# A sorted mixture-of-experts layer: the slot table inverted by one-hot matmuls, token rows gathered straight into SBUF, token weights applied in the combine

## What is computed

```
logits = x @ gate_w.T
scores = jax.nn.softmax(logits, axis=-1)
topk_w, topk_idx = jax.lax.top_k(scores, K)
topk_w = topk_w / jnp.sum(topk_w, axis=-1, keepdims=True)
h = jnp.einsum('th,ehi->eti', x, w1)
g = jnp.einsum('th,ehi->eti', x, w3)
y_all = jnp.einsum('eti,eih->eth', jax.nn.silu(h) * g, w2)
y_sel = y_all[topk_idx, tok]
y = jnp.sum(y_sel * topk_w[..., None], axis=1)
shared = jax.nn.silu(x @ sw1) * (x @ sw3) @ sw2
return (y + shared).reshape(hidden_states.shape)
```

## Time and profile before

| | us |
|---|---|
| median of 3 executions | 1532.87 |
| lowest, highest | 1524.81, 1533.39 |
| the profiled execution, its own time | 1529.62 |
| its span in the trace | 1527.5 |
| PE, DVE, ACT, POOL busy in the span | 1244.4, 954.8, 718.1, 449.8 |

### The profile page before, as it was taken

How to read it: one execution, slowest core, us unless ns; L and a number is a source line. 1 busy time by engine, 2 the same in 40 slices (tenths; PEclk the granted TensorE clock), 3 DMA queues, 4 the chain that set the end, 5 groups by cost and what they waited for, 6 DMA issues and landing times.

```text
span 1527.5 us, 24987 instructions
## 1 busy us (share of the span) xinstructions
PE 1244.4 (81%) x7159; PEld 933.5 (61%) x7195; DVE 954.8 (63%) x2322; ACT 718.1 (47%) x1364; POOL 449.8 (29%) x479
## 2 busy tenths in 40 slices
PE   4579795699765888888869999999789999997466
PEld 3358794577543544545546666666578888885344
DVE  7765454444578999899952445453564555455986
ACT  3452463333336888888842444432423333323275
POOL 3278345200004656565632111210200011003400
PEclk9889897899978999999965999996899999998589
DMA  7645345201011111110100000000000000210001
GB/s 218 124 137 168 111 126 173 62 18 52 1 41 43 42 42 42 42 42 1 35 8 7 8 8 14 0 18 4 21 21 21 21 21 21 87 51 14 1 15 42
DMA packets 72500, 73.36 MB, mean 48 GB/s; under 512 B 10603, under 2 KB 67710, under 8 KB 72414
## 3 DMA queue, kind: packets, MB, share of 16 engines
q1 hardware_dynamic: 69006, 62.98, 14.2%
q0 software_dynamic: 3408, 9.34, 1.7%
HBM read 53.62 MB, written 18.68 MB: 47 GB/s over the span
## 4 chain that ended last, share of the span: by engine, by line
PE 42%; DVE 15%; issue 8%; ACT 6%; POOL 2%; DVEq 0%; ACTq 0%; POOLq 0%
PE bank L935 11%; PE bank L956 5%; PE bank L2505 4%; PE bank L2544 4%; PE bank L2534 3%; DVE work L2041 2%; PE bank L2068 2%; PE bank L2491 2%; DVE work L2031 2%; PE bank L2082 1%; PE bank L2560 1%; DVE resid L2058 1%; PE bank L2075 1%; PE bank L2484 1%; PE bank L2941 1%
## 5 line engine op out<-in xcount | busy, mean ns | idle before, releaser
L2037 POOL TENSOR_TENSOR work<-work 128x512 f32<-128x512 f32 x128 | 163.1, 1275 | 166.6 <-DVE work L2031 166.6
L2068 PE MATMUL bank<-work 128*128 128x512 bf16 x481 | 129.1, 389 | 7.2 <-DVE work L2031 3.8
L2082 PE MATMUL bank<-work 128*128 128x256 bf16 x512 | 78.2, 275 | 38.2 <-ACT work L2025 24.3
L935 PE MATMUL bank<-xhi,whi 128*128 128x512 f32 x256 | 102.2, 399 | 6.1 <-PE bank L956 3.4
L2082 PEld LDWEIGHTS bank<-work 128*128 128x128 bf16 x512 | 41.5, 97 | 100.4 <-issue 96.7
L935 PE MATMUL bank<-xlo,whi 128*128 128x512 f32 x256 | 101.2, 395 | 0.0
L935 PE MATMUL bank<-xhi,wlo 128*128 128x512 f32 x256 | 100.9, 394 | 0.0
L2031 DVE TENSOR_TENSOR work<-work,bank 128x512 f32<-128x512 f32 x128 | 86.4, 676 | 18.6 <-ACT work L2014 15.0
L2020 ACT ACTIVATE work<-work 128x512 f32<-128x512 f32 x128 | 91.7, 716 | 6.0 <-DVE work L2051 5.7
L822 POOL TENSOR_TENSOR wlo<-raw,whi 128x1536 fp32r<-128x1536 f32 x8 | 28.1, 3509 | 224.1 <-ACT whi L836 224.1
L876 DVE TENSOR_TENSOR work<-work,bank 128x512 f32<-128x512 f32 x64 | 44.0, 688 | 78.4 <-PE bank L935 77.6
(11 more groups left out here) (448 smaller groups left out, 3414.1 us busy)
## 6 DMA issues: line engine op xcount, KB each, us to landing
f_got<-f_sorted SPq DMA_DIRECT2D x39, 129.0 KB, 2.1
f_sorted<-clear_row SPq DMA_DIRECT2D x1, 4992.0 KB, 23.5
raw<-in_L_ffn_w SPq DMA_DIRECT2D x24, 176.0 KB
f_back<-f_outputs SPq DMA_DIRECT2D x16, 256.0 KB, 3.0
ctx_in<-in_ctx SPq DMA_DIRECT2D x32, 128.0 KB, 2.0
raw<-in_L_ffn_W SPq DMA_DIRECT2D x14, 256.0 KB, 3.2
f_lines<-f_tokens SPq DMA_DIRECT2D x12, 256.0 KB, 3.7
resid<-in_x SPq DMA_DIRECT2D x4, 512.0 KB, 8.2
```

The source lines that it names most:

```text
L935: mm = pe.matmul(bank[2 * mat + u % 2][0:m, :], up_w(w, slot, mat, c, q), x[:, c, cols], start=j == 0, stop=j == 3 * DC - 1)
L2037: pool.tensor_tensor(prod[:, t % RING, :], once[:, t % 2, :], relu[:, t % RELUS, :], ALU.mult).then_inc(s.prod, 1)
L2068: mm = pe.matmul(bank[2 * m + t % 2][:, :], xqT[:, c, t * P:(t + 1) * P], up_w[:, slot, m, c, :], start=c == 0, stop=c == DC - 1)
L2082: mm = pe.matmul(bank[6 + t % 2][:, 0:D], wholeT[:, t % 2, c * P:(c + 1) * P], down_w[:, slot, c, :], start=c == 0, stop=c == IC - 1)
```

## The change

- The DRAM tensor `f_sorted`, its clearing at the start of the program, the reload of the rows, the payload copies and the 32 scatters into it go.
- VectorE builds a one-hot row matrix [token, 128] and a one-hot column matrix [token, 2 x 39] per choice (`vector_hot`, twice four instructions) after units 2 and 3. TensorE multiplies them (`tensor_inverse`, 32 matmuls, after `tensor_up(5)`). That gives for each of the 39 x 128 slots the token that fills it. VectorE makes from it the source row and the destination row (`vector_slots`, seven small instructions, after unit 5).
- GpSimd gathers the rows of each sorted tile from `f_tokens` straight into a ring of 16 in SBUF (`gather`), 4 in flight: 16 gathers ahead of the tile loop, and one gather behind each of the first 23 scatters in it.
- ScalarE's copy of the output has no weight. The combine has no GpSimd in it: VectorE does two multiply-adds per tile, with the token's weight, in a staggered order.
- The small tables move: GpSimd makes some at the start of the program, VectorE makes others (`vector_tables`) before the first `vector_shift`; the route weights are made after the first `vector_shift` instead of after the fourth. `layer1_weights.load` is issued when the tile loop begins, no longer after its last load.

```
+        def tables_gpsimd(pool):
+            pool.memset(all_one[:, :], 1.0).then_inc(made, 1)
+            pool.iota(count_int[:, :], [[1, P]], base=0, channel_multiplier=0).then_inc(made, 1)
+            pool.iota(row_int[:, :], [[0, 1]], base=1, channel_multiplier=1).then_inc(made, 1)
...
+            def vector_tables(dve):
...
+                link(dve.memset(maskb[:, TILES, :], 0.0))
+                link(dve.tensor_scalar(by_rank, counting[:, 0:E], -1.0, float(E), ALU.mult, ALU.add))
+                link(dve.tensor_scalar(at_tile, counting[:, 0:NT], float(P), None, ALU.mult))
+                link(dve.tensor_scalar(pad_place, at_tile, row1[:, :], float(K * TOK), ALU.add, ALU.add))
...
+                link(dve.tensor_scalar(high, value, (1 - P) / 2.0, 1.0 / P, ALU.add, ALU.mult))
+                link(dve.tensor_scalar(high, high, MAGIC, None, ALU.add))
+                link(dve.tensor_scalar(high, high, MAGIC, None, ALU.subtract))
+                link(dve.scalar_tensor_tensor(low, high, -float(P), value, ALU.mult, ALU.add))
...
+            def vector_hot(dve, k):
+
+                dve.tensor_tensor(rows[k], counting[:, :].unsqueeze(1).to_broadcast([P, TILES, P]),
+                                  low[:, k, :].unsqueeze(2).to_broadcast([P, TILES, P]), ALU.is_equal).then_inc(p.hot, 1)
+                n = [P, TILES, NT]
+                dve.tensor_tensor(columns[k][:, :, 0, :], counting[:, 0:NT].unsqueeze(1).to_broadcast(n), high[:, k, :].unsqueeze(2).to_broadcast(n),
+                                  ALU.is_equal).then_inc(p.hot, 1)
+                dve.wait_ge(p.hot, 4 * k + 2)
+                dve.tensor_tensor(columns[k][:, :, 1, :], columns[k][:, :, 0, :],
+                                  counting[:, k * TILES:(k + 1) * TILES].unsqueeze(2).to_broadcast(n), ALU.mult).then_inc(p.hot, 1)
+                dve.wait_ge(p.hot, 4 * k + 3)
+                dve.tensor_scalar(columns[k][:, :, 0, :], columns[k][:, :, 0, :], row1[:, :], None, ALU.mult).then_inc(p.hot, 1)
...
+            def tensor_inverse(pe):
+                hold(pe, p.hot, 4 * K)
+                for k in range(K):
+                    for t in range(TILES):
+                        mm = pe.matmul(inverse, rows[k][:, t, :], columns[k][:, t, :, :], start=k + t == 0, stop=k == K - 1 and t == TILES - 1)
+                mm.then_inc(p.inverse, 1)
...
+                pool.wait_ge(p.slots, 2)
+                for i in range(2):
+                    pool.wait_ge(p.kept[i], 16 * 2)
+
+                def gather(j):
+                    if j >= FLIGHT:
+                        pool.wait_ge(sent[j % FLIGHT], moved_up_to(j - FLIGHT))
+                    if j >= IN_RING:
+                        pool.wait_ge(s.in_ps, j - IN_RING + 1)
+                    pool.indirect_dma_start(got[:, j % IN_RING, :], None, tokens,
+                                            bass.IndirectOffsetOnAxis(ap=sorter.token[:, j:j + 1], axis=0)).then_inc(sent[j % FLIGHT], 16)
+                for j in range(IN_RING):
+                    gather(j)
                 for j in range(NT):
-                    pool.wait_ge(s.lo, j + 1)
+                    pool.wait_ge(s.out, j + 1)
...
+                    if j + IN_RING < NT:
+                        gather(j + IN_RING)
...
-                        act.activation(y_out[:, i % OUT_RING, :], bank[6 + i % 2][:, 0:D], ACT.Copy,
-                                       scale=got[:, i % IN_RING, D + 1:D + 2]).then_inc(s.out, 1)
+                            act.wait_ge(gone[i % FLIGHT], moved_up_to(i - OUT_RING))
+                        act.activation(y_out[:, i % OUT_RING, :], bank[6 + i % 2][:, 0:D], ACT.Copy).then_inc(s.out, 1)
...
+                for x in range(TILES + K):
+                    for k in range(K):
+                        t = x - k
+                        if 0 <= t < TILES:
+                            if k:
+                                dve.wait_ge(s.acc[k - 1], t + 1)
+                            else:
+                                dve.wait_ge(s.back[t % OUT_RING], 16 * (t // OUT_RING + 1))
+                            dve.scalar_tensor_tensor(X[:, t, :], y_back[:, t % OUT_RING, k, :], sorter.share[:, k, t:t + 1], X[:, t, :],
+                                                     ALU.mult, ALU.add).then_inc(s.acc[k], 1)
+                    if x >= K:
+                        dve.wait_ge(s.acc[K - 1], x - K + 1)
+                        next_stat(dve, x - K)
...
-            steps_at = {1: ("pay", "places"), 3: ("which",), 5: ("powers",), 7: ("series",), 9: ("weights",)}
+            steps_at = {1: ("pay", "places"), 2: ("hot0",), 3: ("hot1",), 5: ("slots", "which"), 7: ("powers",), 8: ("series",), 9: ("weights",)}
```

More of the change, by code:

```diff
@@ L1043, in sorted_experts @@
                 p.up1, p.up2, p.silu, p.hid, p.ahi, p.alo, p.down, p.acc,
-                p.ones, p.mask, p.ranks, p.chain, p.paid, p.where, p.which, p.lined, p.rows0, p.rows1, p.rows2, p.rows3
+                p.mask, p.ranks, p.chain, p.which, p.hot, p.inverse, p.slots
             ) = late.of("kept0 kept1 raw hi0 lo0 stage0 stage1 stage2 hi hi_late lo shift up1 up2 silu hid ahi alo down acc "
-                        "ones mask ranks chain paid where which lined rows0 rows1 rows2 rows3")
-            p.kept, p.stage, p.rows = (p.kept0, p.kept1), (p.stage0, p.stage1, p.stage2), (p.rows0, p.rows1, p.rows2, p.rows3)
@@ L1048, in sorted_experts @@
-            STAGES = 3
+                        "mask ranks chain which hot inverse slots")
+            p.kept, p.stage = (p.kept0, p.kept1), (p.stage0, p.stage1, p.stage2)
             s = Names()
             (
-                s.here0, s.here1, s.here2, s.here3, s.in_ps, s.hi, s.lo, s.up, s.silu, s.act, s.turn_ps, s.ahi, s.alo, s.down, s.out,
-                s.back0, s.back1, s.back2, s.back3, s.pair, s.acc
-            ) = early.of("here0 here1 here2 here3 in_ps hi lo up silu act turn_ps ahi alo down out "
-                         "back0 back1 back2 back3 pair acc")
@@ L1107, in sorted_experts @@
+            columns = [over(f"{name}_columns{k}", work_at, at["columns"][k], [P, TILES, 2, NT], F16)[:, :, :, :] for k in range(K)]
             small, lay = taker(small_area, 512), taker(scratch, at["scratch_size"])
-            pay = small(TILES, K, 2)
-            value, index = small(K, TILES), small(K, TILES, dt=U32)
-            tiles_of, first, end = small(E), small(E), small(E)
-            weights_of, dest = small(NT, dt=I32), small(NT, dt=U32)
             router = make_router(name, split, lay, None, 0, E, K, gate, *router_args, lean=True)
-            logits = router.logits
```

423 lines of the change are left out of this document (204 added, 219 removed).

## The result

The changed kernel takes 1538.6 us (median of 20), the kernel before 1532.6 (median of 20): ratio 1.0039, 95% interval 1.0025 to 1.0054. That is no change by the bound of 1%, and a loss of some 6 us that twenty executions can tell. Forecast 1537.5. Medians are taken over all executions, while ratios and intervals leave out those that ran clearly longer at a lower clock (4 of the 20 after the change), so a ratio isn't always the quotient of the two medians.

What follows compares the result with a forecast made beforehand. TensorE was taken to bound the shared expert and tile loop, a DMA, GpSimd and VectorE chain the combine. Terms summed to +6.95 on the profiled 1529.6, giving 1536.6; forecast put at 1537.5 us, range 1524 to 1551.

Steps and rivals of the forecast that it cites:

- The one-hot matrices: Shared expert: VectorE's wide steps, 4.4 us per choice, make TensorE's `tensor_down(4)` late by +5.9 us.
- The clock in the shared expert: Shared expert: two new TensorE waits of about 2 us, one clock fall taken, +1.3 us, bounds 0 to +2.5.
- From the shared expert to the tile loop: Between shared expert and loop: last scatter and load go, gathers land in time, so the gap goes, -4.4 us.
- The warm clock at loop fill: Loop's start: TensorE idles 1.8 us instead of 6.2, so less low clock, -1.3 us, bounds -2.6 to 0.
- The tile loop: Loop: GpSimd falls behind 0.41 us per tile, 23 times; ring of 4 and TensorE's slack absorb part, +3.1 us.
- The combine: Combine: three-step chain through the ring, 1.39 us a tile against 1.05, +3.3 us, bounds +1 to +5.
- The small tables: Layer's start: GpSimd's low part comes earlier without its seven table operations, -0.95 us, bounds -0.95 to -0.5.
- the start: Up to the shared expert's first up product: earlier by the small tables' -0.95 us.
- the loop's end: From the loop's last copy to the combine's first load back: no change, 0 us.
- Rival (a): Shared expert and loop: wide steps cheap (2.7 us), no clock fall, gathers at 0.95; 1526 us, chance 0.20.
- rival (b): Loop: a gather costing 0.3 us over a scatter's pitch makes GpSimd the bound, +10 us, 1544; chance 0.20.
- Rival (c): Loop: gathers don't get ahead, with landings over 8.5 us; at 12 us, 1547 us; chance 0.03.

Runs made afterwards that it cites:

- the run with four pieces: Changed kernel with the one-hot operations cut into four pieces over units 2 to 5, inverting matmuls two units later: 1535.3 us, ratio to before 1.0024.
- each edit alone: Changed kernel with one edit each: ring of 8 for expert outputs, 1533.0 us; ring of 8 for rows loaded back, 1536.8; one-hot operations in four pieces, 1535.3.
- The combination: Changed kernel with both rings of 8 and the one-hot operations in four pieces, run twice: 1562.6 and 1566.4 us, ratios to before 1.0024 and 1.0081.

## Why the prediction was right, and where it was not

Forecast 1537.5, measured 1538.6. The steps summed to +6.95; the medians differ by 6.0, the layer's end in the two traces by 9.0. By the steps:

- **The one-hot matrices**: right, in mechanism and size. Forecast 2.27, 0.81, 0.81, 0.48; measured 2.28, 0.80, 0.81, 0.39. `tensor_down(4)` came 5.99 later by its distance from the first up product, forecast 5.9. The three runs around it show the cause: the compares' rate can be changed by the layout, and their place in the order is worth 2.9 of the 6. By the Trainium skill's rule named in the prediction (VectorE: DVE Perf Modes, "What auto-detection actually checks") the compare keeps the slow rate, and the trace agrees with 2.28. The estimate from the same rule for the fourth operation was 0.3; it measures 0.39.
- **The clock in the shared expert** (+1.3): wrong, and the step that failed is that a fall of the clock behind the new waits adds to the wait for VectorE. In the change's own execution no clock fell there: the waits were 1.16 ahead of `tensor_down(3)` and 0.46 and 0.64 around the inverting matmuls, not some 2 us, and the granted clock behind them was 1.00. In the run with a ring of 8 for the outputs the first wait was 2.46 and the clock fell to 0.50 behind it, just as forecast; two single executions with the same order (f16 operands, waiting 2.50, and the first one with fewer gathers, 2.51) show the same. But `tensor_down(4)` starts 33.6 to 34.2 after the first up product in all of them, with the fall or without. From unit 1 to unit 4 VectorE, not TensorE, is the bound, and a slower matmul is free there. Behind `tensor_down(4)`, where TensorE is the bound again and a fall would cost, the clock was 1.00 each time. The same holds for another low clock, which the change's execution has earlier. In the trace before it ends with `tensor_down(0)`; here it lasts through most of unit 2 (columns as in the earlier trace rows):

```profile
108.90:112.00 3.10, 3.10 (x10) 2.20 (x10) 2.75 (x12) 0.00 (x0) 0.00 (x0) 0.51 0.00 0
```

Unit 2's up product took 3.99 us against 2.87 before, and that cost nothing here, as the ring-of-8 run shows, but 1.1 in the run with four pieces.
- **From the shared expert to the tile loop** (-4.4): 1.1 too much. The gathers were all in time, but TensorE's first turn still starts 1.19 after the last shared output. I had closed the gap to nothing.
- **The warm clock at loop fill** (-1.3): nothing came in this pair of traces. TensorE idles for 2.9 there instead of 6.2, and the clock was down all the same (0.55). The term has a spread of its own: in the run with a ring of 8 for the outputs, with 3.0 of idle time, the clock was 0.60 and the first copy came after 8.08, 1.1 sooner than before, and with f16 operands after 9.54, 0.4 later. The run with extra matmuls shows that 1.5 to 3.0 are there to be had, if the idle time is filled and not just shortened.
- **The tile loop** (+3.1): the mechanism right (copies released by scatters, from tile 12 where I had said 17, to 27), mis-sized by half. By the forecast's own sum, with the measured 2.58 and 2.11 the lag is 0.46 a tile, 10.7 in 23 tiles, less the 5.1 of the ring 5.6. The 1.2 of slack on TensorE that I subtracted isn't there: ScalarE's program is in order, so that a copy that waits holds the silu of the next tile behind it, and the pitch of TensorE follows at once (2.59). Landings of up to 4.4 us, where I had the usual 2.5, fit the last 0.5: three other executions with the same loop (ring of 8 for the rows back, four pieces, f16 operands) take 84.46, 83.39 and 83.39 from first to last copy, so the loss is 4.9 to 6.1.
- **The combine** (+3.3): 2.78. The three-step chain through a ring of 4 was worth 2.0 (ring-of-8 run); the rest is VectorE's own work.
- **The small tables** (-0.95): GpSimd's low part starts 1.42 earlier, 0.49 of it because the layer began earlier, so 0.93 for the term. The first up product is 2.30 earlier, but its distance from the first statistics is 34.0 to 36.2 in executions of changed kernels (before: 35.8, and 37.5 when profiled again), so the rest can't be told from chance.

The loop came 3.0 longer than forecast, the gap and the warm clock 2.4 less good; the clock in the shared expert (1.2), the start (1.35), the combine (0.5) and the loop's end (0.4) came better. So 5.5 stand against 3.5, and that the total came so near is partly luck. Rival (a) fell with the compares at 2.28 and the gather at its scatter's pitch (0.97 and 0.30); rival (b) fell with the same gather. Rival (c) fell since TensorE waits for no gather anywhere in the loop.

Open: the layer ends 9.0 later in the pair of traces, the medians differ by 6.0. The layer after the change repeats (222.1, and 221.7 with f16 operands), but of before there is one trace on a chip of the first kind. It may simply have been a good one, and 2.2 us of spread ahead of the first up product would explain most of it, but no run here splits it. And no version here was shown to beat the kernel before: on a chip of the first kind each edit alone measured 0.2% to 0.3% over before, where the change has 0.4%, and two of the three intervals reach a tie. The combination ran only on the second kind.

## What to carry to other kernels

When an engine falls behind by a fixed amount per step, ask first how many steps it lasts and what comes after: here a ring twice as deep took back 5 of 6 us of stall without making GpSimd any faster. Don't add two losses before you know that they lie on the same chain; a clock term on an engine that is waiting for another is worth zero, and worth its full length once the wait is gone. And cut long operations of a helper engine to the slack of one unit of its partner: in four pieces of about 2 us instead of two of 4.2 the same work cost 2.9 less.

## What the runs showed of the hardware

- On two of the chips ScalarE and VectorE stood still while GpSimd issued indirect DMAs back to back, up to 31 us at once, although what they waited for was done. On two others they didn't. The kernel before takes 26 to 29 us more on the first two, and a deeper ring, which lets GpSimd run without a break for longer, gains nothing there. What holds the two engines isn't in the trace; that a pause between the issues frees them is read from the loop's profiles and wasn't tried by itself, and ScalarE once went on in the middle of a series.
- A two-tensor operation on f16 data takes 0.475 for 624 elements when no operand has a step of zero in the innermost dimension, and 0.80 when one has. With the zero step 2048 elements take 2.28, as long as the f32 row (2.27).
- Matmuls of 128x78 f16 whose moving operand has a step of 16 elements take 0.30 to 0.32 instead of 0.20, and 32 in a row 4.73 instead of 1.34 (partly at the lower clock).
- Eleven matmuls in a 2.9 us gap kept TensorE's clock up (1.00 instead of 0.50 to 0.60 in the first six microseconds of the loop), worth 1.5 to 3.0 in one execution; shortening the gap from 6.2 to 2.9 was worth between nothing and 1.1.
- A wait of TensorE of 0.94 to 1.51 us ahead of `tensor_down(3)` was followed by a granted clock of 1.00, one of 2.46 to 2.51 by 0.50.
